# A graph network kernel on one core: a reordered preparation, matmuls in front of the attention heads, and normalisations by halves

## The reference

```python
x = _layernorm(x + L0(x, src, dst, ...))            # two attention convolutions, 4 heads
x = _layernorm(x + L1(x, edge_index, edge_weight))  # three GCN convolutions, then h @ Wf + bf
x = _layernorm(x + L2(x, edge_index))               # plain sum over neighbours
x = _layernorm(x + L3(x, edge_index, edge_attr_32)) # two edge convolutions, batch norm behind each

def _gat_conv(x, src, dst, W, al, ar, b, act):      # in L0, once with tanh, once without
    z = (x @ W).reshape(N, H, F)
    e = leaky_relu(sum(z * al)[src] + sum(z * ar)[dst], 0.2)
    alpha = softmax of e over the edges of each dst
    return act(segment_sum(z[src] * alpha, dst) + b)

def _egnn_conv(...):                                # in L3
    h = x @ W + b
    return relu(segment_sum(h[src] + edge_emb, dst) + h) + bias

def _batchnorm(x, gamma, beta):                     # over the nodes, per feature
    return (x - mean(x)) * rsqrt(var(x) + 1e-5) * gamma + beta
```

## Time and profile before

| | us |
|---|---|
| median of 3 runs | 7297.76 (7267.9 to 7310.4) |
| the profiled execution | 7296.74 |
| its span, first to last instruction | 7295.1 |
| PE busy | 4543.0 (62%) |
| DVE busy | 4165.7 (57%) |
| ACT busy | 2134.5 (29%) |
| POOL busy | 3458.1 (47%) |

### The profile page before, as it was taken

How to read it: one execution, slowest core, us unless ns; L and a number is a source line. 1 busy time by engine, 2 the same in 40 slices (tenths; PEclk the granted TensorE clock), 3 DMA queues, 4 the chain that set the end, 5 groups by cost and what they waited for, 6 DMA issues and landing times.

```text
span 7295.1 us, 121057 instructions
## 1 busy us (share of the span) xinstructions
PE 4543.0 (62%) x28553; PEld 2993.0 (41%) x28553; DVE 4165.7 (57%) x13273; ACT 2134.5 (29%) x5938; POOL 3458.1 (47%) x4137
## 2 busy tenths in 40 slices
PE   1565666666566565444555555555578888888865
PEld 1233333333333344222222322333377777677754
DVE  4677677687787663666566676667661111224344
ACT  0444355454454431333333333333310000000000
POOL 2777767777677603777777777777500000000000
PEclk9676667676776665666666666666659999999988
DMA  5455455455555532444444544444439899899966
GB/s 93 128 147 157 123 155 160 140 155 157 139 156 146 151 99 56 118 128 121 129 127 121 136 135 131 129 133 134 138 138 415 356 396 416 340 416 399 371 284 251
DMA packets 934340, 1390.68 MB, mean 191 GB/s; under 512 B 483496, under 2 KB 689474, under 8 KB 917769
## 3 DMA queue, kind: packets, MB, share of 16 engines
q1 hardware_dynamic: 687776, 912.42, 36.9%
q0 software_dynamic: 128976, 222.12, 12.3%
q10 hardware_dynamic: 117332, 253.47, 9.3%
HBM read 1014.16 MB, written 373.27 MB: 190 GB/s over the span
## 4 chain that ended last, share of the span: by engine, by line
issue 23%; SPq 18%; DVE 16%; PE 15%; DMA 14%; DVEq 5%; ACT 4%; another core or an unknown queue 2%; POOL 2%; ACTq 1%; POOLq 0%
DMA arena<-adj_w_d 8%; SPq L520 4%; DMA arena<-adj_c_d 4%; SPq L499 4%; DVE arena L1020 3%; SPq L486 3%; PE bank L1756 3%; PE bank L1757 3%; PE bank L1760 2%; PE bank L1718 2%; ACT arena L1891 2%; POOL arena L800 2%; SPq L501 2%; DVE arena L1043 1%
## 5 line engine op out<-in xcount | busy, mean ns | idle before, releaser
L800 POOL DMA_INDIRECT arena<-table_d,arena x3136 | 3135.1, 1000 | 1353.6 <-issue 1125.6
L1612 PE MATMUL bank<-arena 128*128 128x500 f16 x3750 | 1355.4, 501 | 1109.3 <-issue 639.4
L1633 PE MATMUL bank<-arena 128*65 128x40 f32 x7500 | 742.5, 255 | 880.4 <-issue 667.6
L1612 PEld LDWEIGHTS bank<-arena 128*128 128x128 f16 x3750 | 431.3, 123 | 1826.5 <-issue 1561.4
L1891 ACT ACTIVATE arena<-arena 128x128 f16<-128x128 f16 x3750 | 1122.7, 396 | 85.0 <-DVEq L1121 55.3
L1633 PEld LDWEIGHTS bank<-arena 128*65 128x65 f32 x7500 | 671.2, 169 | 1022.6 <-issue 851.2
L1756 PE MATMUL bank<-arena 125*128 125x250 f16 x3750 | 859.3, 274 | 156.1 <-DMA arena<-adj_w_d 132.9
L1757 PE MATMUL bank<-arena 125*128 125x250 f16 x3750 | 855.5, 273 | 0.0
L1020 DVE TENSOR_SCALAR arena<-arena 128x500 f16<-128x500 f16 x1875 | 689.0, 367 | 214.7 <-issue 118.6
L1614 PE MATMUL bank<-arena 128*128 128x500 f16 x1875 | 681.6, 471 | 68.6 <-issue 66.3
L1106 DVE SCALAR_TENSOR_TENSOR arena<-arena,bank 128x250 f16<-128x250 f16 x1250 | 455.3, 411 | 441.2 <-issue 330.3
(11 more groups left out here) (244 smaller groups left out, 4326.2 us busy)
## 6 DMA issues: line engine op xcount, KB each, us to landing
arena<-adj_w_d SPq DMA_DIRECT2D x720, 625.0 KB, 10.9
arena<-adj_c_d SPq DMA_DIRECT2D x345, 625.0 KB, 11.5
adj_w_d<-arena ACTq DMA_DIRECT2D x125, 1250.0 KB
arena<-msg_d SPq DMA_DIRECT2D x1250, 103.5 KB
msg_d<-arena POOLq DMA_DIRECT2D x196, 552.0 KB
adj_c_d<-arena ACTq DMA_DIRECT2D x125, 625.0 KB
arena<-table_d,arena POOLq DMA_INDIRECT x3136
arena<-in_edge_features SPq DMA_DIRECT2D x625, 51.0 KB
```

The lines of the kernel that those rows point to most:

```text
L800: g_.indirect_dma_start(ring[:, i, k * XC:(k + 1) * XC], None, table_d, bass.IndirectOffsetOnAxis(ap=idx_cur[:, i, k:k + 1], axis=0)).then ...
L1612: mm(wb, lhsT=row_oh[:, slot, c, i, :], rhs=col_oh[:, slot, c, :], start=(c == 0 and i == 0), stop=(c == CH - 1 and i == 1))
L1633: last = mm(out, lhsT=rows_sl[:, g, w, c, 0:AGG], rhs=grh[:, g, w * CH + c, :], start=(c == 0), stop=(c == CH - 1))
```

## The change

It has four parts.

1. **Preparation.** DVE makes the row indices, then the table, then the offsets, and last the records. POOL waits for the indices (`idx_made`) in place of the records. The table is stored by ACT, ahead of `er_d`. SP stores the offsets before the records. PE makes the table's 50 products before the two small ones for the largest edge weight.
2. **Attention, both layers.** `keep_busy` puts matmuls with 500 columns of 2-byte numbers in front of the head products, 12 before the first block and 6 before each other; the heads overwrite their result.
3. **First normalisation.** The scale is taken from a bound, the largest `dinv` times 8, and `layer_norm`, `xin` and the split are done half by half, so also ACT's square root.
4. **Batch norms.** Each block adds its sums and squares, taken around the first block's mean row, so `batch_norm_factors` works on 64 numbers in a partition, and scale and shift become one multiplication and one addition (`batch_norm_half`). The scale of n = 5 is taken from a bound on gamma and beta, made in `per_node_weights_vector`; `top_scale` is left out there. The last layer norm and the store of the output go by halves. (`LN_BLOCKS` only counts the square roots, which are one more; `bconv` has 128 rows in place of 125.)

```diff
 def prep_sync(sp):
...
-    sp.wait_ge(s("prep_step"), PREP["rec_made"])
-    sp.dma_start(rec_d.rearrange("(j p c) f -> p j (c f)", p=P, c=BK), rec_all.rearrange("p (j c) f -> p j (c f)", c=BK)).then_inc(s("rec_stored"), 16)
     sp.wait_ge(s("prep_step"), PREP["ptr_made"])
...
     sp.dma_start(ptr_d[:, NW:NW + 1], ptr_end).then_inc(s("items_out"), 16)
+    sp.wait_ge(s("prep_step"), PREP["rec_made"])
+    sp.dma_start(rec_d.rearrange("(j p c) f -> p j (c f)", p=P, c=BK), rec_all.rearrange("p (j c) f -> p j (c f)", c=BK)).then_inc(s("rec_stored"), 16)
     sp.wait_ge(s("items_out"), 64)
...
-    sp.wait_ge(s("table_made"), 1)
-    sp.dma_start(table_rows(), xt).then_inc(s("table_stored"), 16)
...
-            pool.wait_ge(s("prep_step"), PREP["rec_made"])
+            pool.wait_ge(s("prep_step"), PREP["idx_made"])
...
 def prep_tensor(pe):
     pe.wait_ge(s("consts_made"), 1)
-    pe.wait_ge(s("prep_step"), PREP["ew_max"])
-    mm(bank[6][0:1, 0:P], lhsT=ews[:, 3:4], rhs=ident, start=True, stop=True).then_inc(s("top_xt"), 1)
...
     pe.wait_ge(s("xT_loaded"), 16)
     pe.wait_ge(s("prep_step"), PREP["v_made"])
     for t in range(T):
         last = mm(bank[7][0:NT, t * 2 * H:(t + 1) * 2 * H], lhsT=xT_sb[:, t * NT:(t + 1) * NT], rhs=vw[:, 0, :], start=True, stop=True)
     last.then_inc(s("el_psum"), 1)
+    pe.wait_ge(s("prep_step"), PREP["ew_max"])
+    mm(bank[6][0:1, 0:P], lhsT=ews[:, 3:4], rhs=ident, start=True, stop=True).then_inc(s("top_xt"), 1)
...
...
+def keep_busy(out, count):
+    for _ in range(count):
+        mm(out[:, 0:T * WN], lhsT=iota_lo, rhs=iota_key, start=True, stop=True)
...
             def heads(i, u):
                 pe.wait_ge(agg_loaded[u], i * 16 + 16 * (layer * (B // NG) + 1))
                 wait_some(pe, s("gat_y"), i * NG + (u + base - 1))
+                keep_busy(gat_banks(u)[0], 12 if first(i) and u == 0 else 6)
...
+                if layer == 0:
+                    act.dma_start(table_rows(), xt).then_inc(s("table_stored"), 16)
                 act.dma_start(nodes(er_d), er_sb).then_inc(s("er_stored"), 16)
...
-            layer_norm(d)
-
-            v.tensor_tensor(xin, x_sb, bc(dinv, 2, F), ALU.mult)
-            d.drain()
+            top_scale(d, 0)
+            for h in halves(0):
+                t = half(h)
+                layer_norm(d, t)
+                v.tensor_tensor(xin[:, t, :], x_sb[:, t, :], bc(dinv[:, t], 2, F), ALU.mult)
+                d.drain()
+                parts_half(d, 0, xin, t)
...
-            parts_vector(d, 0, xin)
...
 def post(b, par, k, foremost=False):
...
-    v.tensor_reduce(stat[:, 5, :], x_out[:, t2, :].rearrange("p t f -> p f t"), AX.X, ALU.add)
+    v.tensor_tensor(yc, x_out[:, t2, :], bc(stat[:, 6, :], 1, 2), ALU.subtract)
     d.drain()
-    v.tensor_tensor(stat[:, 0, :], stat[:, 0, :], stat[:, 5, :], ALU.add)
+    v.tensor_tensor(yd[:, 0:2, :], yc, yc, ALU.mult)
+    v.tensor_tensor(yd[:, 2, :], yc[:, 0, :], yc[:, 1, :], ALU.add)
+    d.drain()
+    v.tensor_tensor(yd[:, 0, :], yd[:, 0, :], yd[:, 1, :], ALU.add)
+    v.tensor_tensor(stat[:, 7, :], stat[:, 7, :], yd[:, 2, :], ALU.add)
+    d.drain()
+    v.tensor_tensor(stat[:, 5, :], stat[:, 5, :], yd[:, 0, :], ALU.add)
     d.drain()
...
-            batch_norm(d, hout, 0)
-            parts_vector(d, 5, hout)
+            batch_norm_factors(d, 0)
+            for h in halves(5):
+                batch_norm_half(d, hout, half(h))
+                parts_half(d, 5, hout, half(h))
...
-            batch_norm(d, xin, 1)
-            v.tensor_tensor(x_sb, x_sb, xin, ALU.add)
-            d.drain()
-            layer_norm(d)
-            d.drain().then_inc(s("cv_done"), 1)
+            batch_norm_factors(d, 1)
+            for h in range(2):
+                t = half(h)
+                batch_norm_half(d, xin, t)
+                v.tensor_tensor(x_sb[:, t, :], x_sb[:, t, :], xin[:, t, :], ALU.add)
+                d.drain()
+                layer_norm(d, t)
+                d.sem_inc(s("cv_done"), 1)
```

164 lines of the change are left out of this document (102 added, 62 removed).

## The result

| | median us | runs | lowest to highest |
|---|---|---|---|
| before | 7303.28 | 20 | 7247.89 to 7334.24 |
| after | 7238.50 | 20 | 7216.54 to 7292.88 |

The ratio is 0.9923, 95% interval 0.9907 to 0.9939: 65 us faster by the medians, where 92.5 were forecast. The profiled execution of after has a span of 7242.3, 52.8 under the 7295.1 of before. The time lies in the wide range given (7175 to 7246), but above the forecast's own (7188 to 7222), and nearer to the rival "the waiting moves elsewhere" (7243) than to 7205. Not all of that rival's reasons hold, as the runs show.

A forecast was written before the change was run, and what follows sets the result against it. Bounds: a preparation chain, DVE, POOL and DMAs alternating in windows, the adjacency stream in convolutions, DVE in normalisations. Gains 20 + 28 + 1 + 9.5 + 18 + 16 = 92.5 off 7296.7 gave 7205 us; 8-in-10 range 7175 to 7246.

The forecast's parts named there:

- the waiting moves elsewhere: Rival: POOL's head start worth nothing, records cancel the order's gain, attention hand-over 4.6 us; 7243 us; 19 in 100.
- preparation and first groups: Preparation and start of layer 0's windows: lists 6 us earlier plus 14 of DVE's waits, 20 gained, between -5 and 39.
- attention, layer 0: Wide matmuls lift PE's clock; block period 5.51 to 4.15 us over 24 blocks, 28 gained, between 20 and 32.
- attention, layer 1: PE's gain stops at DVE's pace: 5.5 less 4.2 for the first twelve matmuls, 1 us, between -4 and 3.
- first normalisation: Before the first convolution: work by halves lets PE and the stream start sooner, 9.5 us gained, between 5 and 14.
- between the convolutions 4 and 5: Batch norm step: PE starts 23 us earlier, the first slot comes free 18 earlier; 18 gained, between 15 and 21.
- the end: Last sum to end of span: halves and overlapped store, 49.0 us in place of 65.2; 16 gained, between 13 and 18.
- The lists' step: Preparation: offsets' stores leave at 66.4, records at 80.8, lists back at 107.5 in place of 113.17; 6 us gained.
- the lists' half of this as a rival: Rival: offsets' stores slow ACT's table store, POOL starts near 110, lists 10 late; 7234 us; 5 in 100.
- a start of the windows behind 157: Sign of being wrong: layer 0's first window was expected at about 151 us, against 157.40 before.
- two early waits of DVE: Windows of layer 0: of 16.7 us and about 10 more waiting, 14 would be gained, between 0 and 27.
- the clock doesn't hold: Rival: clock not held in the attention, adding 130 us; 7363 us, slower than before; 5 in 100.

The follow-up runs named there:

- after_again: The unchanged kernel after, run again in another series beside before; 7121.06 us, 0.9913 of before.
- dense_only: The kernel before with only the halved first normalisation, the batch norms from running sums and the halved output; 7168.57 us, 0.9963 of before.
- prep_only: The kernel before with only the reordered preparation; 7168.67 us, 0.9963 of before.
- pad140: The kernel after with 140 extra DVE drains at the end of the preparation; 7117.97 us, 0.9889 of before.
- pad8: The kernel after with 8 extra DVE drains ahead of the third convolution's loop; 7105.02 us, 0.9869 of before.
- before_pad32: The kernel before with 32 extra DVE drains ahead of the third convolution's loop; 7206.96 us, 1.0015 of before.
- after_third: The unchanged kernel after, run once more as the base of the last series; 7297.67 us, 0.9923 of before.
- keep_l1_only: The kernel before with the wide matmuls ahead of the heads in layer 1 alone; 7332.14 us, 1.0012 of before.
- keep_l0: The kernel after with the wide matmuls ahead of the heads in layer 0 only; 7115.40 us, 0.9887 of before.
- keep3: The kernel after with three wide matmuls in place of six, in layer 0 alone; 7298.37 us, 0.9975 of before.
- combined: The kernel after with offsets made and loaded back earlier, 8 drains ahead of n = 2, wide matmuls in layer 0 alone; 7223.59 us, 0.9867 of before.

## Why the prediction was right or wrong

| term | predicted | measured |
|---|---|---|
| preparation and first groups | 20 | 27.1, 27.0 and 28.6 in three series, 12.6 and 13.2 in two others |
| attention, layer 0 | 28 | 24.3 and 25.2 |
| windows, layer 1 | not seen | -12.6 in the profiles of before and after, about -2 in after_again |
| attention, layer 1 | 1 | 1.0 in after (0 to 2.5 where the clock holds), about -25 where it falls |
| first normalisation | 9.5 | 9.5 and 9.1 |
| third convolution | not seen | -13.0 and -10.6 |
| between the convolutions 4 and 5 (from the start of the fourth convolution to PE's last matmul) | 18 | 16.1 and 17.2 |
| the end (from PE's last matmul) | 16 | 14.9 and 15.0 |

For the two profiles the measured terms add up: 12.6 + 24.3 - 12.6 + 1.0 + 9.5 - 13.0 + 16.1 + 14.9 = 52.8. Of the 39.7 us that are missing from 92.5, the two stages that the sum held at nothing have 25.6. The medians of 20 executions are 64.8 apart, 27.7 short; how these 27.7 divide no profile shows, but the third convolution's 10 to 13 are in every profile of the change. So the step that failed first of all is a term that the sum left out, the third convolution. Beside it one step, one term's base and one condition were wrong.

**The lists' step failed.** I had the offsets' stores leave at 66.4 and be done before the records at 80.8, and the lists' input at 107.5 (80.8 + 24 + 3 make 107.8). In fact the four-byte stores crawled beside ACT's two stores, the table and `er_d` (10.13, 5.66 and 10.10 us to issue), the records left at 93.19, and the loads behind them blocked SP for 23.19: 131.92. In before the same four had taken 28.4 us beside the records (12.59, 4.25, 3.21 and 8.30, L434 to L437), and I took that for the records' doing, which the new order would end; ACT's stores took their place, and `er_d`, of which I had said that nobody needs it before the windows, was beside the later ones in both kernels. My bound (records of 35 us: 5 lost) left the stores' own time untouched. I had named the lists' half of this as a rival, with the opposite for POOL (start near 110, where it was 78.78), 10 late, and gave it 5 in 100; they were 19 late, and a start of the windows behind 157 was one of my own signs of being wrong. It cost less than it should have, since the other half of my reasoning was wrong too: not two early waits of DVE seem to decide, but POOL. From its first gather to its last in layer 0 it needs 24.5 us a block in dense_only, with blocks 24.6 apart even at the start of after (107.54 and 132.12), so it hardly rests, and a start 50 earlier (78.8 against 129.2) less a pause of 19 would be worth 31, where prep_only's last gather comes 27.5 earlier. This is argued and only half tested: the third series, where POOL needs 25.1 to 25.3 a block, has 28.6, the last one, with 25.3 to 25.7, has 13.2, and taking the pause away gave 3 to 4 us in one and 30 in the other.

**Attention of layer 0: the base.** The period of after is 4.17 in most blocks and 4.15 on average, as forecast. But I multiplied the gain by 24 periods of 5.51, and before has only 21 of them: its first three blocks' heads run one behind the other in 10.31 us, and from the first to the last block's heads there are 127.0 us and not 132.2. So the term was 5.2 too large there; the last block's shorter heads gave 1.8 back, and the first twelve matmuls cost 4.7 (4.2 forecast): 24.3 were left. The 0.21 us that the sum takes for a wide matmul was an estimate, and after has it at a clock of 0.98 over the stage: six take 1.28 us from the first to the heads behind them (2700.82 to 2702.10). At the clock of 0.50 six take 2.50 in pad140 (5200.16 to 5202.66 us), 0.417 each, so the 5.0 for the first twelve fits too.

**Not in the sum: code.** I held the convolutions' own stages at nothing because the diff doesn't touch them. I counted instructions that DVE executes, not where the others come to lie. With 35 more ahead of it a loop of 273 starts at 2866 in place of 2831: 10.4 to 13 us, shown from both sides by pad8 and before_pad32.

**Not in the sum: the windows of layer 1.** In the two profiles they took back 12.6 us, in after_again about 2. The cause is open; that the stage differs by 22 us among the profiles of the slower series (2435.8 to 2458.0) suggests that it belongs to the execution more than to the change.

**The clock of layer 1.** The rival "the clock doesn't hold" was put at 5 in 100 for both layers at once and for whole executions. Its 130 us of loss, 2.5 a block from six matmuls at the low clock in both layers, are in no run: no profiled execution with these matmuls was low throughout even one layer. It is a part of the rival that came: in layer 1 alone, from the middle of the stage, in some executions. For a gain of 0 to 2.5 us the matmuls there put 25 at risk: three of the eight profiles with them show the fall (pad140, after_third and keep_l1_only). Two of six executions of after_again took 24 to 42 us longer than the others' median, which fits, but they have no profile. That PE is never idle, my argument against, was true of layer 0 and not of layer 1, where DVE sets the pace at the high clock: this stood in my own numbers (4.0 for DVE). But it protects less than I thought, since layer 0 had its own falls of about 10 us in pad8 and keep_l0. Nor do idle times of PE decide an execution: PE was 93 and 89% busy ahead of the falls in pad140 and keep3, and just as busy (93%) in pad8, where the clock held.

The rest held closely: the first small product at 49.13 (49.0), POOL's first row at 78.78 (81), PE's start 24.9 behind the last attention block (24) and its second half 16.5 behind the first, the step between the convolutions 13.4 (14.1), the end 48.9 (49.0). So the rival "the waiting moves elsewhere" had the right time and mostly other reasons: the first normalisation and the gap between the convolutions gave nearly all that was forecast, and the hand-over in layer 0 was 4.17 and not 4.6.

## What to carry to other kernels

Where a change adds instructions ahead of a long loop, look at that loop's own stage afterwards, even if the change leaves it alone; a pause of several us put down to "issue" right behind a loop's jump, with packets on the instruction queue, was the sign here (6.4 to 6.6 us). A few drains ahead of the loop cured it for one loop (273 instructions, 8 drains, 10.4 us) and not for another (392, 140 drains). Matmuls that only hold the clock paid in layer 0 (24.3 and 25.2 us), where PE was the bound even at the high clock (busy for 100.48 of 101 us in after); in layer 1, where DVE was then the bound, they gained 0 to 2.5 us, and a fall in some executions cost 25. Small stores that others wait for are best sent ahead of other stores on every queue, not only on their own: here they took 7.4 us to issue alone and 26.2 beside those of another queue. And one profile on each side is a weak base for a sum by stages: a stage that neither kernel changes differed here by 12.6 us. Several kernels of one series, each with a part of the change, gave each stage a base.

## What the runs showed of the hardware

- Pauses of DVE at a loop's jump, with packets on the instruction queue: 6.4 to 6.6 us and once more 3.9 to 4.7 beside a stream of 398 GB/s (n = 2, eight profiles), 3.4 to 5.1 at the lighter load of the windows of layer 0 (about 150 GB/s; before and pad140).
- The granted clock in the attention of layer 0: with three 500-column matmuls ahead of sixteen instructions of 4-byte products 1.00 for 20 us and then 0.50 for 100 (keep3); with six 1.00 for most of 101 us, but 0.51 for 10 us in the middle in keep_l0. With the 4-byte products alone 0.50 throughout, PE being busy for 103.00 of 103 us (layer 1 in keep_l0).
- The same four stores in runs of four bytes took SP 7.4 us to issue alone (combined), 26.2 beside a 1.7 MB store and one of 6250 rows of 16 bytes on another queue (after), and 28.4 behind a 3.9 MB store on their own queue, with the same small rows beside them (before).
